# Routing logits by column tiles, one coefficient transpose and an earlier turn of the rows in the second mixture of experts

## The chip, the cores and the metric

The kernel runs on one core of one Trainium2 chip. The metric is device microseconds of one execution. Five engines run their own instruction streams side by side and wait for each other on semaphores: TensorE (PE, with its weight loads shown apart as PEld), VectorE (DVE), ScalarE (ACT), GpSimd (POOL) and SyncE (SP), which issues the transfers.

## The reference

Four layers, each a gated cross-attention and a gated feed-forward block, act on x of 128 sequences of 64 rows of 128 features. The change lies in the feed-forward block of the third layer, a mixture of 8 experts with hidden width 192 of which each row takes two:

```python
xn = _layernorm(x)
logits = xn @ Wr + br
probs = softmax(logits)
topk_probs, topk_idx = top_k(probs, 2)
combine = sum_k topk_probs[:, k] * one_hot(topk_idx[:, k], 8)
for ei in range(8):
    h = gelu(xn @ W1[ei] + b1[ei])
    y = h @ W2[ei] + b2[ei]
    out = out + combine[:, ei:ei + 1] * y
x = x + tanh(g_ffn[2]) * out
```

All 8 experts are computed for every row, and the coefficients (zero but for two) weigh them.

## The kernel before, in words

The 8192 rows lie in SBUF as 64 tiles of 128 rows. Eight stages follow each other, and the stage here, `experts2`, takes the rows in 16 groups of four tiles (512 rows). It is software-pipelined by hand: `steps` runs a body for steps -3 to 15, in which `at(0)` is the group whose outputs are made (g), `at(1)` the one whose hidden units are made (nxt), `at(2)` the one that is routed (far), and `at(3)` the one that is normalised (new). Each engine has such a body, and the order of its instructions is the order in the text.

For one group TensorE does this:

- It turns the four normalised tiles into PSUM (`t_front`, L737). ACT copies the 512 columns into `xTg` (`a_front`, L742).
- Logits (L1667): the turned rows are the weights, the 8 columns of the router's matrix move, once for each tile.
- Hidden units (`hidden`, L1645): 12 chunks of 128 units for 512 rows, three in each quarter of the body. ACT applies gelu (L1808).
- Coefficients: DVE makes scores, softmax, the two best and the coefficients (`scores` and `routing`, L1699 to L1724). PE turns them to 8 rows of 512 in four transposes (L1684), ACT copies them (L1827), SP stores them to DRAM (L1621) and loads them spread over all 128 partitions (L1625, `wide_coef`).
- Weighing: DVE multiplies the hidden units by the spread coefficients (`weigh`, L1736).
- Biases: four matmuls of the 8 turned coefficients by the second biases (L1689), which DVE adds to the rows (`biased`, L1750).
- Outputs (`outputs`, L1655): 12 matmuls for each tile, one tile in each quarter. DVE adds them to the rows (L1782).

On TensorE the quarters of a body are hidden, outputs, hidden, outputs and so on; the logits of far stand ahead of the first quarter, the transposes of its coefficients behind the second outputs, its bias matmuls behind the third, and `t_front` of new behind the fourth. In float32 each matmul shows as two records in the profile, and a transpose as one.

On DVE the body is: scores of far, the outputs of the last group added to x, statistics of new, the first three chunks weighed, new normalised (L205), routing of far, and the other chunks weighed with the bias addition among them. In one step, for far = group 8, `weights3` runs on DVE at the end as well: it unpacks weights of the last stage (L372 to L385).

At the start of a stage each engine waits until the stage before it has updated all its rows. The first steps (`opening` on DVE) have an order of their own.

Stages elsewhere in the kernel that the prediction reads rows from: L485 multiplies 64x64 pieces of weights in `attention0`, with four pieces at different rows and columns of the array; `experts0` (L947, L856) weighs the first mixture with a spread that lies by tiles.

Of the kernel before, what the change touches and what calls it, by code (L numbers as in the profile page):

```python
# [12 lines left out]
ALU = mybir.AluOpType  # L13
ACT = mybir.ActivationFunctionType
AX = mybir.AxisListType
F32 = mybir.dt.float32
# [4 lines left out]
P = 128  # L21
# [60 lines left out]
class Transfers:  # L82
# [6 lines left out]
    def at(self, t):  # L89
        return self.sems[t.par]  # L90
# [1499 lines left out]
def experts2(k, no):  # L1590
# [2 lines left out]
    k.stage_memory()  # L1593
    xTg = [k.take(GCOLS) for _ in range(2)]
    hT = [v.rearrange("p (c n) -> p c n", c=CHUNKS2) for v in (k.take(CHUNKS2 * GCOLS) for _ in range(2))]
    wide_coef = [v.rearrange("p (e n) -> p e n", e=EXPERTS) for v in (k.take(EXPERTS * GCOLS) for _ in range(2))]
    small = lambda: k.take(GROUP * EXPERTS).rearrange("p (j e) -> p j e", j=GROUP)
    score, shifted, expd, hits, coef = small(), small(), small(), small(), small()
    route = Route(k)
    smax, ssum, srec = k.take(GROUP), k.take(GROUP), k.take(GROUP)  # L1600
    coefT = k.take(GCOLS)
    weights3 = Dequantised(k)
    HALF = P // 2
    SCALED = 2 * EXPERTS
    XT, LOGITS, COEFT, HID, NHID, OUT = 0, 1, 2, 3, 3, 6
    s = k.sigs(G, dict(
        l_psum=1, score=1, smax=1, shifted=1, expd=1, ssum=1, srec=1, routing_prob=1, hits=1, coef=1, ct_psum=1,
        ct_sb=1, b2_psum=1, b2_added=1, h_psum=CHUNKS2, h_sb=CHUNKS2, scaled=SCALED, out_psum=1))
    coef_dram = k.nc.dram_tensor("coef_scratch", [G, EXPERTS, GCOLS], F32, kind="Internal").ap()
    coef_stored, coef_spread = k.transfers(G, "coef_stored"), k.transfers(G, "coef_spread")  # L1610
    d_front, p_front, t_front, a_front = group_front(k, f, xTg, XT)
    wide = [P, GROUP, EXPERTS]
# [2 lines left out]
        return k.x[:, bass.ds(g.idx * GROUP, GROUP), :].rearrange("p j n -> p (j n)")  # L1615

    def sync(sp):
        def body(at):
            if g := at(2):
                sp.wait_ge(*s["ct_sb"](g))  # L1620
                sp.dma_start(coef_dram[g.idx], coefT[0:EXPERTS, :]).then_inc(coef_stored.at(g), 16)  # L1621
                sp.wait_ge(*coef_stored(g))
                if g.has(2):
                    sp.wait_ge(*s["scaled"](g.back(2)))
                sp.dma_start(wide_coef[g.par].rearrange("p e n -> p (e n)"),  # L1625
                             coef_dram[g.idx].rearrange("e n -> (e n)").partition_broadcast(P))\
                    .then_inc(coef_spread.at(g), 16)
        steps(sp, G, 2, 0, body)

# [6 lines left out]
    def tensor(pe):  # L1636
        def hidden(g, first):

            for c in range(first, first + 3):
                if c >= NHID:  # L1640
                    pe.wait_ge(*s["h_sb"](g, c - NHID + 1))
                elif g.has(1):
                    pe.wait_ge(*s["h_sb"](g.back(1), CHUNKS2 - NHID + c + 1))
                w = k.w1s[:, c, 0:P] if c < EXPERTS else k.w1tail[:, c - EXPERTS, :]
                pe.matmul(ps[:, HID + c % NHID, :], w, xTg[g.par], start=True, stop=True).then_inc(s["h_psum"].sem, 1)  # L1645

        def outputs(g, j):

            if j == 0 and g.has(2):
                pe.wait_ge(*f["x_updated"](sub(g.back(2), GROUP - 1)))  # L1650
            for c in range(CHUNKS2):
                if j == 0:
                    pe.wait_ge(*s["scaled"](g, c + 1 if c < EXPERTS else EXPERTS + 2 * (c - EXPERTS + 1)))
                w = k.w2a[:, c, :] if c < EXPERTS else k.w2b[:, c - EXPERTS, :]
                mm = pe.matmul(ps[:, OUT + g.par, j * D:(j + 1) * D], hT[g.par][:, c, j * P:(j + 1) * P], w,  # L1655
                               start=c == 0, stop=c == CHUNKS2 - 1)
            if j == GROUP - 1:
                mm.then_inc(s["out_psum"].sem, 1)

        def body(at):  # L1660
            g, nxt, far = at(0), at(1), at(2)
            if far:
                pe.wait_ge(*f["xT_sb"](far))
                if far.has(1):
                    pe.wait_ge(*s["b2_added"](far.back(1)))
                for j in range(GROUP):
                    mm = pe.matmul(ps[:, LOGITS, j * EXPERTS:(j + 1) * EXPERTS], xTg[far.par][:, j * P:(j + 1) * P],  # L1667
                                   k.wr2[:, :], start=True, stop=True)
                mm.then_inc(s["l_psum"].sem, 1)
            if at(3) and not nxt:  # L1670
                t_front(pe, at(3))
            if far and far.idx == 0:
                hidden(far, 0)
            for q in range(GROUP):
                if nxt and (q or nxt.idx):
                    hidden(nxt, 3 * q)
                if g:
                    outputs(g, q)
                if far and q == 1:
                    pe.wait_ge(*s["coef"](far))  # L1680
                    if far.has(1):
                        pe.wait_ge(*s["ct_sb"](far.back(1)))
                    for j in range(GROUP):
                        mm = pe.transpose(ps[0:EXPERTS, COEFT, j * P:(j + 1) * P], coef[:, j], k.ident)  # L1684
                    mm.then_inc(s["ct_psum"].sem, 1)
                if far and q == 2:
                    pe.wait_ge(*s["ct_sb"](far))
                    for j in range(GROUP):
                        mm = pe.matmul(ps[:, LOGITS, j * D:(j + 1) * D], coefT[0:EXPERTS, j * P:(j + 1) * P],  # L1689
                                       k.b2r[:, :], start=True, stop=True)  # L1690
                    mm.then_inc(s["b2_psum"].sem, 1)
            if at(3) and nxt:
                t_front(pe, at(3))
        steps(pe, G, 3, 0, body)

    def vector(dve):
        def scores(g):
            dve.wait_ge(*s["l_psum"](g))
            dve.tensor_tensor(score, ps[:, LOGITS, 0:GROUP * EXPERTS].rearrange("p (j e) -> p j e", j=GROUP),  # L1699
                              k.br2[:, :].unsqueeze(1).broadcast_to(wide), ALU.add).then_inc(s["score"].sem, 1)  # L1700
            dve.wait_ge(*s["score"](g))
            dve.tensor_reduce(smax, score, AX.X, ALU.max).then_inc(s["smax"].sem, 1)
            dve.wait_ge(*s["smax"](g))
            dve.tensor_tensor(shifted, score, smax.unsqueeze(2).broadcast_to(wide), ALU.subtract)\
                .then_inc(s["shifted"].sem, 1)
# [21 lines left out]
        def weigh(g, first):  # L1727

            for c in range(first, first + 3):
                dve.wait_ge(*s["h_sb"](g, c + 1))  # L1730
                if c < EXPERTS:
                    parts = [(slice(0, P), c)]
                else:
                    parts = [(slice(h * HALF, h * HALF + HALF), 2 * (c - EXPERTS) + h) for h in range(2)]
                for rows, e in parts:
                    dve.tensor_tensor(hT[g.par][rows, c, :], hT[g.par][rows, c, :], wide_coef[g.par][rows, e, :],  # L1736
                                      ALU.mult).then_inc(s["scaled"].sem, 1)

        def statistics(g):
            for j in range(GROUP):  # L1740
# [31 lines left out]
        def body(at):  # L1772
            old, nxt, far, new = at(-1), at(1), at(2), at(3)
            if not at(0) and not old:
                opening(at)
                return
            if far:
                scores(far)
            if old:
                dve.wait_ge(*s["out_psum"](old))  # L1780
                dve.wait_ge(*s["b2_added"](old))
                dve.tensor_tensor(rows_of(old), ps[:, OUT + old.par, :], rows_of(old), ALU.add)\  # L1782
                    .then_inc(f["x_updated"].sem, GROUP)
            if new:
                statistics(new)
            if nxt:
                dve.wait_ge(*coef_spread(nxt))
                weigh(nxt, 0)
            if new:
                normalised(new)  # L1790
            if far:
                routing(far)
            if nxt:
                weigh(nxt, 3)
                weigh(nxt, 6)
            if far:
                biased(far)
            if nxt:
                weigh(nxt, 9)
            if far and far.idx == G // 2:  # L1800
                weights3.vector(dve)
        steps(dve, G, 3, 1, body)

    def scalar(act):
# [5 lines left out]

        def body(at):
            nxt, far = at(1), at(2)
            for q in range(GROUP):
                if nxt and (q or nxt.idx):
                    hidden_out(nxt, 3 * q)
# [6 lines left out]
                if far and q == 2:  # L1822
                    act.wait_ge(*s["ct_psum"](far))
                    if far.has(1):
                        act.wait_ge(*coef_stored(far.back(1)))
                        act.wait_ge(*s["b2_psum"](far.back(1)))
                    act.activation(coefT[0:EXPERTS, :], ps[0:EXPERTS, COEFT, :], ACT.Copy).then_inc(s["ct_sb"].sem, 1)  # L1827
            if at(3) and (nxt or not far):
                a_front(act, at(3))
        steps(act, G, 3, 0, body)  # L1830
# [421 lines left out]
```

## Time and profile before

| what | value |
|---|---|
| median of 3 runs | 2160.76 us (2160.32 to 2162.66) |
| the profiled execution's own time | 2156.8 us |
| its span | 2155.0 us |
| TensorE busy | 1918.2 us, 89% |
| VectorE busy | 1670.9 us, 78% |
| ScalarE busy | 1297.6 us, 60% |
| GpSimd busy | 263.6 us, 12% |

The busy share is an average over all eight stages. The stage of the change lies between 1302 and 1717 us of the span, so it is 415 of 2155 us. The median of the runs is 4.0 us above the profiled execution.

### The profile page before, as it was taken

To read this page: it belongs to the slowest core of one execution; us is meant where nothing else is said; L and a number is where in the kernel's file an instruction comes from. 1 tells how busy PE (TensorE), PEld (TensorE's weight loads), DVE (VectorE), ACT (ScalarE), POOL (GpSimd) and SP (SyncE) were. 2 spreads that over 40 slices of the span, in tenths; PEclk is the share of its full clock that TensorE was granted. 3 is DMA by queue.
4 is the path that set the end of the run, shared out by engine and by line. 5 is a ranking of instruction groups with operands and counts; after the bars stand their busy time and mean duration, and the time that the engine had idled before them with its cause. 6 is when DMAs were issued, how large, how long until landed. Compare 5 with 4: busy or idle time off the path is not lost. (4 is left out here: it accounts for less than half of the span.)

```text
span 2155.0 us, 48493 instructions
## 1 busy us (share of the span) xinstructions
PE 1918.2 (89%) x17841; PEld 1473.2 (68%) x17841; DVE 1670.9 (78%) x4752; ACT 1297.6 (60%) x3151; POOL 263.6 (12%) x551
## 2 busy tenths in 40 slices
PE   7999999999969999999999797999999994699608
PEld 6777787787759987777767575777677773344208
DVE  6787787787759979999867797667766488787894
ACT  5777777777742238888866464444455265218744
POOL 1111111111111111111111241000000022100000
PEclk9999999999969999999999898999999997799859
DMA  5222221111125621111100111222222110002452
GB/s 156 52 65 59 53 57 46 44 46 42 42 99 222 237 94 33 33 32 32 24 1 1 30 50 79 80 103 95 79 79 80 50 50 21 0 0 103 179 187 79
DMA packets 115148, 151.60 MB, mean 70 GB/s; under 512 B 45657, under 2 KB 96354, under 8 KB 110818
## 3 DMA queue, kind: packets, MB, share of 16 engines
q1 hardware_dynamic: 111730, 146.91, 21.1%
q8 instruction: 145, 2.38, 0.5%
q10 hardware_dynamic: 3184, 1.58, 0.3%
q14 instruction: 89, 0.73, 0.1%
HBM read 110.18 MB, written 21.50 MB: 61 GB/s over the span
## 5 line engine op out<-in xcount | busy, mean ns | idle before, releaser
L1808 ACT ACTIVATE arena<-banks,b1c 128x512 f32<-128x512 f32 x192 | 131.9, 687 | 166.4 <-PE banks L1645 166.2
L1736 DVE TENSOR_TENSOR arena<-arena 128x512 f32<-128x512 f32 (+1 forms) x256 | 170.5, 686 | 61.5 <-ACT arena L1808 56.4
L624 ACT ACTIVATE arena<-banks,arena 128x128 f32<-128x128 f32 x512 | 180.6, 373 | 1.3 <-DVE arena L570 1.3
L1655 PEld LDWEIGHTS banks<-w2a,arena 128*128 128x128 f32 x1024 | 124.1, 192 | 28.7 <-issue 28.7
L496 PE MATMUL banks<-arena,wk 128*128 128x128 f32 x1024 | 134.0, 285 | 1.2 <-DVE arena L594 1.2
L876 PE MATMUL banks<-we,arena 128*128 128x128 f32 x1024 | 131.5, 285 | 1.5 <-DVE arena L947 0.2
L535 PE MATMUL banks<-wv,arena 128*128 128x512 f32 x256 | 131.9, 597 | 0.0
L496 PEld LDWEIGHTS banks<-arena,wk 128*128 128x128 f32 x1024 | 121.7, 195 | 12.5 <-issue 10.8
L876 PEld LDWEIGHTS banks<-we,arena 128*128 128x128 f32 x1024 | 122.8, 197 | 7.0 <-DVE arena L947 6.2
L1655 PE MATMUL banks<-w2a,arena 128*128 128x128 f32 x1024 | 124.7, 275 | 0.0
L541 PEld LDWEIGHTS banks<-konst,arena 128*128 128x128 f32 x512 | 59.1, 141 | 93.6 <-DVE arena L552 59.0
L1645 PE MATMUL banks<-arena,w1s 128*128 128x512 f32 x256 | 121.8, 609 | 0.0
L624 ACT ACTIVATION_READ_ACCUMULATOR arena<-banks,arena 128x1 f32 x512 | 109.5, 214 | 0.0
L205 DVE TENSOR_SCALAR xhat<-x_tiles,mean_var,rstd 128x128 f32<-128x128 f32 x256 | 79.2, 341 | 34.3 <-POOL rstd L729 27.7
L726 POOL TENSOR_SCALAR var_eps<-mean_var 128x4 f32<-128x4 f32 x96 | 22.1, 231 | 682.3 <-DVE mean_var L706 680.1
L570 DVE TENSOR_REDUCE arena<-banks 128x4 f32<-128x512 f32 x128 | 82.5, 686 | 29.4 <-PE banks L485 29.4
L729 POOL TENSOR_TENSOR rstd<-var_eps,konst 128x4 f32<-128x4 f32 x96 | 100.5, 1047 | 15.2 <-POOL var_eps L726 10.6
L632 ACT ACTIVATE arena<-banks 128x512 f32<-128x512 f32 x64 | 38.2, 597 | 104.0 <-PE banks L496 104.0
L1904 PE MATMUL banks<-konst,local_max 128*1 128x128 f32 (+1 forms) x4 | 1.4, 347 | 111.6 <-DVE local_max L1888 111.6
L552 DVE TENSOR_TENSOR arena<-arena 128x512 f32<-128x512 f32 x128 | 88.6, 692 | 4.4
L541 PE MATMUL banks<-konst,arena 128*128 128x128 f32 x512 | 80.4, 280 | 12.8 <-DVE arena L552 12.7
L1197 ACT ACTIVATE arena<-arena 128x512 f32<-128x512 f32 x128 | 80.7, 630 | 15.9 <-DVE arena L1151 11.4
(246 smaller groups left out, 5023.5 us busy)
## 6 DMA issues: line engine op xcount, KB each, us to landing
arena<-coef_scratch SPq DMA_DIRECT2D x32, 2048.0 KB, 7.2
arena<-arena SPq DMA_DIRECT2D x256, 64.0 KB, 2.0
gated_scratch<-arena SPq DMA_DIRECT2D x16, 768.0 KB, 3.3
arena<-gated_scratch SPq DMA_DIRECT2D x16, 768.0 KB, 4.4
arena<-z1T_scratch SPq DMA_DIRECT2D x128, 64.0 KB, 2.3
arena<-in_ctx_turned SPq DMA_DIRECT2D x32, 256.0 KB, 2.9
arena<-in_ctx SPq DMA_DIRECT2D x64, 64.0 KB, 2.1
z1T_scratch<-arena SPq DMA_DIRECT2D x64, 64.0 KB, 1.6
```

Of the source, the lines that this page charges most:

```text
L496: mm = pe.matmul(ps[:, n, c * P:(c + 1) * P], k.wk0[:, c * P:(c + 1) * P], Z[t.idx % 3][:, :, n], start=True, stop=True)
L535: pe.matmul(ps[:, V0 + b, :], Z[t.idx % 3][:, b].rearrange("p s i -> p (s i)"), k.wv0[:, :], start=True, stop=True).then_inc(s["v_psum"].s ...
L541: mm = pe.transpose(ps[:, b, c * P:(c + 1) * P], prob[:, b, c * P:(c + 1) * P], k.ident)
L552: dve.tensor_tensor(each, each, rec[:, o].unsqueeze(2).broadcast_to([P, HPAIRS, P]), ALU.mult)\
L570: dve.tensor_reduce(low[:, o], ps[:, SCORES + o, :].rearrange("p (c n) -> p c n", c=HPAIRS), AX.X, ALU.max, negate=True).then_inc(s["low"] ...
L624: act.activation(prob[:, o, c * P:(c + 1) * P], ps[:, SCORES + o, c * P:(c + 1) * P], ACT.Exp, bias=low[:, o, c:c + 1], accum_out=total[:, ...
L729: pool.tensor_tensor(k.rstd[:, :, 0], k.ve[:, :, 0], k.konst[:, C_MHALF:C_MHALF + GROUP], ALU.pow).then_inc(f["rstd_ready"].sem, GROUP)
L876: mm = pe.matmul(ps[:, OUT + g.par, j * D:(j + 1) * D], xs[g.par][:, n, j * P:(j + 1) * P], k.we0[:, n, :], start=n == 0, stop=n == EXPERT ...
L1645: pe.matmul(ps[:, HID + c % NHID, :], w, xTg[g.par], start=True, stop=True).then_inc(s["h_psum"].sem, 1)
L1655: mm = pe.matmul(ps[:, OUT + g.par, j * D:(j + 1) * D], hT[g.par][:, c, j * P:(j + 1) * P], w, start=c == 0, stop=c == CHUNKS2 - 1)
L1736: dve.tensor_tensor(hT[g.par][rows, c, :], hT[g.par][rows, c, :], wide_coef[g.par][rows, e, :], ALU.mult).then_inc(s["scaled"].sem, 1)
L1808: act.activation(hT[g.par][:, c, :], ps[:, HID + c % NHID, :], ACT.Gelu, bias=k.b1c[:, c:c + 1])\
```

## The change

Router logits: the router's matrix, widened with zeros to 32 columns (`wr_roomy`), becomes the weights and 128 turned rows move. The four tiles of a group go to four column strips of the array, 32 output partitions each, so that the logits come out turned: expert by row. ACT copies the 128x128 block to SBUF, and a new transpose (`logits_turned`) on PE brings it back to rows by experts. This transpose stands behind the first hidden quarter.

Coefficients: DVE writes them into a 128x128 block (`roomy`) with 32 columns for each tile, whose other columns stay zero. One transpose turns all four tiles.

Biases: `b2_blocks` holds the biases four times on a block diagonal, so that one matmul of 512 columns makes all four tiles. It is filled by four transfers at the stage's start, after DVE has cleared it.

The rows of new are turned ahead of the fourth outputs rather than behind them. On DVE the scores move behind the update of x and the statistics. The store of the coefficients has 128 rows of 512 bytes, and the spread reads four pieces of 4 KB for each partition. The clears and a copy run on DVE at the start of the stage.

```diff
-    wide_coef = [v.rearrange("p (e n) -> p e n", e=EXPERTS) for v in ...]
+    wide_coef = [v.rearrange("p (j e n) -> p e j n", j=GROUP, e=EXPERTS) for v in ...]
+    ROOM = P // GROUP
+    roomy = k.take(P)
+    coef = roomy.rearrange("p (j e) -> p j e", j=GROUP)[:, :, 0:EXPERTS]
+    wr_roomy = k.take(ROOM)
+    b2_blocks = k.take(GCOLS)
+    logitsT = k.take(P)
-    coefT = k.take(GCOLS)
+    coefT = k.take(P)
...
     def sync(sp):
+        sp.wait_ge(cleared, 4)
+        for j in range(GROUP):
+            sp.dma_start(b2_blocks[j * ROOM:j * ROOM + EXPERTS, j * D:(j + 1) * D], k.a["L2_ffn_b2"])\
+                .then_inc(b2_loaded, 16)
...
-                sp.dma_start(coef_dram[g.idx], coefT[0:EXPERTS, :]).then_inc(coef_stored.at(g), 16)
+                sp.dma_start(coef_dram[g.idx], coefT).then_inc(coef_stored.at(g), 16)
...
-                sp.dma_start(wide_coef[g.par].rearrange("p e n -> p (e n)"),
-                             coef_dram[g.idx].rearrange("e n -> (e n)").partition_broadcast(P))\
+                sp.dma_start(wide_coef[g.par].rearrange("p e j n -> p j e n"),
+                             coef_dram[g.idx].rearrange("(j e) n -> j e n", j=GROUP)[:, 0:EXPERTS].partition_broadcast(P))\
...
+        def logits_turned(g):
+            pe.wait_ge(*s["lt_sb"](g))
+            pe.transpose(ps[:, LOGITS, P:2 * P], logitsT, k.ident).then_inc(s["l_psum"].sem, 1)
+
+        pe.wait_ge(cleared, 4)
+        pe.wait_ge(b2_loaded, 16 * GROUP)
...
-                    mm = pe.matmul(ps[:, LOGITS, j * EXPERTS:(j + 1) * EXPERTS], xTg[far.par][:, j * P:(j + 1) * P],
-                                   k.wr2[:, :], start=True, stop=True)
-                mm.then_inc(s["l_psum"].sem, 1)
+                    mm = pe.matmul(ps[j * ROOM:(j + 1) * ROOM, LOGITS, 0:P], wr_roomy, xTg[far.par][:, j * P:(j + 1) * P],
+                                   start=True, stop=True)
+                mm.then_inc(s["lt_psum"].sem, 1)
+                if not nxt:
+                    logits_turned(far)
...
                 if nxt and (q or nxt.idx):
                     hidden(nxt, 3 * q)
+                if far and nxt and q == 0:
+                    logits_turned(far)
+                if nxt and at(3) and q == GROUP - 1:
+                    t_front(pe, at(3))
                 if g:
                     outputs(g, q)
...
-                    for j in range(GROUP):
-                        mm = pe.transpose(ps[0:EXPERTS, COEFT, j * P:(j + 1) * P], coef[:, j], k.ident)
-                    mm.then_inc(s["ct_psum"].sem, 1)
+                    pe.transpose(ps[:, COEFT, 0:P], roomy, k.ident).then_inc(s["ct_psum"].sem, 1)
                 if far and q == 2:
                     pe.wait_ge(*s["ct_sb"](far))
-                    for j in range(GROUP):
-                        mm = pe.matmul(ps[:, LOGITS, j * D:(j + 1) * D], coefT[0:EXPERTS, j * P:(j + 1) * P],
-                                       k.b2r[:, :], start=True, stop=True)
-                    mm.then_inc(s["b2_psum"].sem, 1)
-            if at(3) and nxt:
-                t_front(pe, at(3))
+                    pe.matmul(ps[:, LOGITS, :], coefT, b2_blocks, start=True, stop=True).then_inc(s["b2_psum"].sem, 1)
...
     def vector(dve):
+        dve.memset(roomy, 0.0).then_inc(cleared, 1)
+        dve.memset(b2_blocks, 0.0).then_inc(cleared, 1)
+        dve.memset(wr_roomy, 0.0).then_inc(cleared, 1)
+        dve.wait_ge(cleared, 3)
+        dve.tensor_copy(wr_roomy[:, 0:EXPERTS], k.wr2[:, :]).then_inc(cleared, 1)
+        dve.wait_ge(cleared, 4)
...
-            dve.tensor_tensor(score, ps[:, LOGITS, 0:GROUP * EXPERTS].rearrange("p (j e) -> p j e", j=GROUP),
+            dve.tensor_tensor(score, ps[:, LOGITS, P:2 * P].rearrange("p (j e) -> p j e", j=GROUP)[:, :, 0:EXPERTS],
...
-                    dve.tensor_tensor(hT[g.par][rows, c, :], hT[g.par][rows, c, :], wide_coef[g.par][rows, e, :],
-                                      ALU.mult).then_inc(s["scaled"].sem, 1)
+                    by_tile = hT[g.par][rows, c, :].rearrange("p (j n) -> p j n", j=GROUP)
+                    dve.tensor_tensor(by_tile, by_tile, wide_coef[g.par][rows, e], ALU.mult).then_inc(s["scaled"].sem, 1)
...
-            if far:
-                scores(far)
             if old:
...
             if new:
                 statistics(new)
+            if far:
+                scores(far)
...
             nxt, far = at(1), at(2)
+            if far:
+                act.wait_ge(*s["lt_psum"](far))
+                act.activation(logitsT, ps[:, LOGITS, 0:P], ACT.Copy).then_inc(s["lt_sb"].sem, 1)
...
-                    act.activation(coefT[0:EXPERTS, :], ps[0:EXPERTS, COEFT, :], ACT.Copy).then_inc(s["ct_sb"].sem, 1)
+                    act.activation(coefT, ps[:, COEFT, 0:P], ACT.Copy).then_inc(s["ct_sb"].sem, 1)
```

## Rows read from the trace of the kernel before

**Rows 1.** Windows of the stage: busy time and records by engine, granted clock, DMA:

```profile
1440.00:1465.00 25.00, 24.31 (x145) 18.02 (x144) 16.99 (x53) 12.09 (x18) 1.69 (x2) 1.00 0.21 86
```

**Rows 2.** Timeline of PE over one group: start, busy, line, [idle before]:

```profile
1432.98 1.06 PE L1667 MATMUL banks<-wr,arena 128*128 128x8 f32 x8 [0.69 <-ACT arena L742]
1433.90 2.82 PE L1645 MATMUL banks<-arena,w1s 128*128 128x512 f32 x6
1436.56 1.95 PE L1655 MATMUL banks<-w2a,arena 128*128 128x128 f32 x16
...
1444.49 0.60 PE L1684 MATMUL banks<-konst,arena 128*8 128x128 f32 x4
1444.93 1.88 PE L1645 MATMUL banks<-arena,w1s 128*128 128x512 f32 x4
...
1447.50 1.95 PE L1655 MATMUL banks<-w2a,arena 128*128 128x128 f32 x16
...
1450.27 1.15 PE L1689 MATMUL banks<-b2r,arena 8*128 8x128 f32 x8
1451.36 2.84 PE L1645 MATMUL banks<-arena,w1tail 128*128 128x512 f32 x6
1454.04 1.95 PE L1655 MATMUL banks<-w2a,arena 128*128 128x128 f32 x16
...
1456.71 0.60 PE L737 MATMUL banks<-konst,xhat 128*128 128x128 f32 x4
1458.00 1.06 PE L1667 MATMUL banks<-wr,arena 128*128 128x8 f32 x8 [0.69 <-ACT arena L742]
```

**Rows 3.** Timeline of PE in the first attention, around L485:

```profile
405.09 0.45 PE L485 MATMUL banks<-arena 64*64 64x128 f32 x8
```

**Rows 4.** The same, a longer stretch:

```profile
405.09 1.10 PE L485 MATMUL banks<-arena 64*64 64x128 f32 x32
406.12 2.05 PE L496 MATMUL banks<-arena,wk 128*128 128x128 f32 x16
```

**Rows 5.** Timeline of DVE over the same group as rows 2:

```profile
1434.08 0.19 DVE L1699 TENSOR_TENSOR arena<-banks,br 128x32 f32<-128x32 f32 x1 [1.58 <-PE banks L1667]
...
1434.64 0.69 DVE L1782 TENSOR_TENSOR x_tiles<-banks,x_tiles 128x512 f32<-128x512 f32 x1
...
1436.55 1.86 DVE L1736 TENSOR_TENSOR arena<-arena 128x512 f32<-128x512 f32 x3
1438.79 1.12 DVE L205 TENSOR_SCALAR xhat<-x_tiles,mean_var,rstd 128x128 f32<-128x128 f32 x4 [0.37 <-POOL rstd L729]
...
1442.54 0.25 DVE L1724 SCALAR_TENSOR_TENSOR arena<-arena,gates 128x32 f32<-128x32 f32 x1
```

**Rows 6.** Timeline of ACT, end of the same group:

```profile
1454.24 0.69 ACT L1808 ACTIVATE arena<-banks,b1c 128x512 f32<-128x512 f32 x1 [0.17 <-PE banks L1645]
1457.35 0.60 ACT L742 ACTIVATE arena<-banks 128x512 f32<-128x512 f32 x1 [2.43 <-PE banks L737]
```

**Rows 7.** Groups of instructions by line, costliest first, of DVE, POOL and ACT:

```profile
L1207 ACT ACTIVATE arena<-banks 128x128 f32<-128x128 f32 x64 | 17.8, 277 | 9.8 <-PE banks L1091 9.3
...
L1424 POOL MEMSET arena<- 128x512 f32 x4 | 2.0, 528 | 101.7 <-DVE x_tiles L1782 75.8 <-DVE x_tiles L1327 25.9
```

**Rows 8.** One line's instructions, L947: duration min/median/max in ns:

```profile
L947 DVE TENSOR_TENSOR arena<-arena x128: 680/684/693, 635.4 to 776.5; 128x512 f32<-128x512 f32 x128
```

**Rows 9.** Timeline of SP, the spread of the same group:

```profile
1450.35 0.33 SPq L1625 DMA_DIRECT2D arena<-coef_scratch  x1
```

**Rows 10.** DMA issues: tiles, count, KB each, median us to landing:

```profile
arena<-coef_scratch SPq DMA_DIRECT2D x32, 2048.0 KB, 7.2
...
out_x<-x_tiles SPq DMA_DIRECT2D x4, 1024.0 KB, 5.1
```

**Rows 11.** Timeline of PE after the step with the unpacking of weights:

```profile
1522.11 0.60 PE L1684 MATMUL banks<-konst,arena 128*8 128x128 f32 x4 [2.41 <-DVE arena L1724]
```

**Rows 12.** Timeline of DVE in the opening, the first weighing:

```profile
1324.50 1.89 DVE L1736 TENSOR_TENSOR arena<-arena 128x512 f32<-128x512 f32 x3 [1.45 <-DMA arena<-coef_scratch]
```

More of the change, by code:

```diff
@@ L1595, in experts2 @@
     hT = [v.rearrange("p (c n) -> p c n", c=CHUNKS2) for v in (k.take(CHUNKS2 * GCOLS) for _ in range(2))]
-    wide_coef = [v.rearrange("p (e n) -> p e n", e=EXPERTS) for v in (k.take(EXPERTS * GCOLS) for _ in range(2))]
+    wide_coef = [v.rearrange("p (j e n) -> p e j n", j=GROUP, e=EXPERTS) for v in (k.take(EXPERTS * GCOLS) for _ in range(2))]
     small = lambda: k.take(GROUP * EXPERTS).rearrange("p (j e) -> p j e", j=GROUP)
-    score, shifted, expd, hits, coef = small(), small(), small(), small(), small()
+    score, shifted, expd, hits = small(), small(), small(), small()
+    ROOM = P // GROUP
[4 more added lines that the diff above has]
+    logitsT = k.take(P)
     route = Route(k)
     smax, ssum, srec = k.take(GROUP), k.take(GROUP), k.take(GROUP)
-    coefT = k.take(GCOLS)
+    coefT = k.take(P)
     weights3 = Dequantised(k)
@@ L1606, in experts2 @@
     s = k.sigs(G, dict(
-        l_psum=1, score=1, smax=1, shifted=1, expd=1, ssum=1, srec=1, routing_prob=1, hits=1, coef=1, ct_psum=1,
+        lt_psum=1, lt_sb=1, l_psum=1, score=1, smax=1, shifted=1, expd=1, ssum=1, srec=1, routing_prob=1, hits=1, coef=1, ct_psum=1,
         ct_sb=1, b2_psum=1, b2_added=1, h_psum=CHUNKS2, h_sb=CHUNKS2, scaled=SCALED, out_psum=1))
-    coef_dram = k.nc.dram_tensor("coef_scratch", [G, EXPERTS, GCOLS], F32, kind="Internal").ap()
+    cleared, b2_loaded = k.sem("L2_cleared"), k.sem("L2_biases_loaded")
+    coef_dram = k.nc.dram_tensor("coef_scratch", [G, P, P], F32, kind="Internal").ap()
     coef_stored, coef_spread = k.transfers(G, "coef_stored"), k.transfers(G, "coef_spread")
```

## The prediction

> **What bounds the kernel now.** I read the windows first, to see which engine sets the pace of this stage. In the 25 us from 1440 TensorE is busy for 24.31 us at granted clock 1.00 (2.4 GHz), VectorE for 17.0 and ScalarE for 12.1 [rows 1]. The other windows between 1340 and 1640 us look the same but for one, so PE sets the pace and a microsecond off PE's stream is one off the group. Next comes PE's timeline over one group, from logits to logits: 1432.98 to 1458.00, or 25.02 us [rows 2]. I take it apart by the starts of its blocks. Three hidden chunks with nothing odd beside them take 2.57 us (1444.93 to 1447.50), and outputs of one tile 2.67 (1454.04 to 1456.71). Four of each make 21.0 us, which the change leaves alone. The other 4.0 us are what it works on:
>
> - logits: 0.92 us, and the hidden quarter behind them takes 2.66 rather than 2.57; together 1.00;
> - the four transposes of coefficients: 0.44;
> - the bias matmuls: 1.09, with 0.10 more in the outputs ahead (1447.50 to 1450.27) and 0.11 in the hidden quarter behind (1451.36 to 1454.04); together 1.30;
> - the turned rows: 1.29 from the transposes at 1456.71 to the logits at 1458.00, of which 0.69 is the wait for ACT's copy, named in the last row of the group.
>
> Last come DVE's and ACT's timelines, for what else could be late: DVE waits 1.58 us for the logits [rows 5], and ACT's copy has an idle ahead of it, waiting for PE [rows 6].
>
> **The change part by part.**
>
> The turned rows. The four transposes stay; four in a row cost 0.44 (the coefficients' four in [rows 2]). Moved ahead of the fourth outputs, they leave 2.67 us of outputs to hide the copy. ACT is then in the last gelus: the last starts 0.20 us and ends 0.89 us after the hidden quarter (1454.24 plus 0.69, against 1454.04), and the copy takes 0.60 [rows 6]; it ends some 1.6 us after the hidden quarter, while PE arrives at the logits after 0.44 + 2.67 = 3.1 us. So 1.29 becomes 0.44: 0.85 saved. If only the named wait went, it would be 0.69. New's normalised rows are ready at 1439.9 (1438.79 plus 1.12, [rows 5]), long before. Behind the moved transposes stand only the outputs, whose operands are ready. 13 steps (0 to 12) have this slot.
>
> The coefficients. One transpose instead of four: 0.11 for 0.44, 0.33 saved in 14 steps (0 to 13). The three that go have no other effect, and the weight is 128 columns wide as in the turned rows, which cost 0.11 as well.
>
> The biases. One matmul of 512 columns is two records; six take 2.57, so two 0.86. The slot was 1.30, so 0.44 saved in 14 steps. The bounds: 0.2 if the small extras on either side stay, 0.44 if they go. I take the upper end, since such an extra shows beside every block with a narrow tile in this group and beside no full one.
>
> The logits. Eight records again, of 128 columns instead of 8. One after another at 0.11 they would take 0.88. The nearest row to four strips of the array at once is L485: eight records of 128 columns each, on four pieces of the array, span 0.45 us from the first start to the last end [rows 3], where eight starts 0.11 apart would span more than 0.88. 32 of them take 1.03 us to the next block's start [rows 4], 0.032 each; in batches of four that start 0.107 apart, eight batches are 0.86, and 0.17 is left as the price of going in and out. Eight records in strips are then two batches, 0.21, with 0.17 and about 0.1 in the quarter beside them: 0.5. To this comes one transpose, 0.11. So 1.00 becomes 0.61: 0.39 saved in 14 steps. The bounds are 0.36 (saves 0.64) and, if the strips run one after another, 0.88 + 0.28 + 0.11 = 1.27 (loses 0.27). I stay near L485, since a strip differs from its pieces only in depth.
>
> A rule of the Trainium skill speaks against this part: by TensorEngine Tiling (Array Packing), section Instruction Overhead, a matmul costs about 60 cycles however few columns move. The old eight records of 8 columns would be 0.2 us by it (an estimate: 8 times 60 cycles at 2.4 GHz), less than the new ones, and the logits would lose 0.33 a group instead of saving 0.39, a sum of 15.2 instead of 25.3. The trace has 0.92 for them [rows 2], so the rule's price isn't theirs here; their 128-column weights have to be loaded.
>
> The copy of the turned logits on ACT is new: 0.28 by a copy of that size [rows 7]. ACT has 12.9 us of idle in 25 [rows 1], and does it while PE is in the first hidden chunk, 0.86 us long. The new transpose waits for it only behind three chunks.
>
> The scores come later. They start 2.48 us before the second block, the outputs at 1436.56 [rows 2, 5]; the transpose now ends at that block, so they start about 0.2 after it begins, 2.7 later. In exchange the update of x and the statistics (1434.64 to 1436.55, 1.91 us) run ahead of them, in the idle of 1.58 and beyond, and the 0.37 for GpSimd's rstd goes [rows 5]. The coefficients are thus 0.4 later against PE. They were ready at 1442.79, 1.70 before their transpose at 1444.49; 1.3 us of slack stay. Costed at nothing; without the cover every microsecond costs one.
>
> Weighing. Its third operand is now read in four pieces. The first mixture does just this in 684 ns [rows 8]; here three took 1.86 [rows 5]. Nothing.
>
> The spread. Four pieces of 4 KB a partition instead of one of 16. It was issued at 1450.35 and lands 7.2 later, at 1457.6 [rows 9, 10]; DVE first reads it a group on, at 1461.6. By the new order DVE reads it 15.9 after the coefficients' transpose rather than 17.1, so 2.8 us of slack stay. The longest that the pieces make it: out_x moves 1024 KB in 512-byte pieces in 5.1 us [rows 10], so 2048 KB in 10.2. That would eat it and 0.2 of the slack above. Nothing, in steady state.
>
> The opening. Three clears and a copy on DVE come before the first statistics. A clear of 512 columns took 0.53 on GpSimd [rows 7]; I take 1.1 for the four with their waits, 0.5 to 1.5 as bounds. SP issues four loads of biases behind them, and PE waits for these before its first transposes, which wait for about 4 us of normalising anyway. The opening ends with the first spread, for which DVE waits [rows 12]; it comes 1.1 later, PE's shorter blocks give a little back. 1.0 lost, and 3 more if the spread in pieces takes as long as out_x makes possible.
>
> The step after the unpacking. There PE waits 2.41 us for coefficients [rows 11]. DVE sets that step's end, so what PE saves on the way (0.85 and 0.39) is not gained, but for the 0.37 of rstd: about 1.0 lost.
>
> The sum: 13 x 0.85 = 11.1; 14 x (0.33 + 0.44 + 0.39) = 16.2; less 1.0 and 1.0: 25.3 us. The profiled execution took 2156.8 us, so 2131.5 for one like it; the median of the runs lies 4.0 above it, which gives 2135.5.
>
> **The rivals.**
>
> *The strips run one after another.* For: nothing here shows weights 128 rows deep and 32 columns wide in strips. Against: [rows 3], with eight records in 0.45. The logits lose 0.27 instead of saving 0.39, 14 x 0.66 = 9.2: 2144.7.
>
> *The copy still comes late.* If ACT reaches it only after the fourth outputs, the 0.85 stays: 2135.5 + 11.1 = 2146.6. Against: the 1.5 us between the copy's end and PE's arrival. This would be the change not doing what it says.
>
> *DVE takes over.* If scores to coefficients take 2 us longer than I make it, 0.7 a group goes past the slack, 9 us over 13 groups: 2144.6. For: 1.3 us is the tightest slack here. Against: every piece of the chain has its row.
>
> *The spread late, the one that ends slower.* The slacks of the spread and the coefficients add up to 4.1 us, so landing above 11.3 us costs a microsecond a group; from 13.3 (25.3 over 13 is 1.95) the kernel is slower than before. At 14 it is 2.7 x 13 = 35 lost: 2170.6. For: four times the pieces. Against: out_x's 10.2.
>
> **How the numbers follow.** Measurement tells a difference of about 0.2% (4.3 us) from none. I give my forecast 0.71, its own range 2130 to 2143; the strips 0.11, the late copy 0.04, DVE 0.07, the late spread 0.04, and 0.03 that several shortfalls meet within 0.2%. Faster 0.93, same 0.03, slower 0.04. The range: at the low end the logits at 0.36 (3.5 more) and an opening at nothing (1.0 more), 2131, with 2 us for the median's scatter, 2129; at the high end the strips and the late copy, 2147.
>
> **What would show it.** The turned rows' block ahead of the fourth outputs with no wait at the logits; a group of 23.0 us; the logits' block at about 0.5; two bias records in 0.86; PE with no wait for L1724's coefficients but in the step after the unpacking, there about 3.3 us. The prediction is wrong if a wait for coefficients or for the spread shows in every group, or if the logits' eight records start 0.11 apart.

## The result and the profile after

The changed kernel takes 2142.5 us (median of 4 runs, 2140.7 to 2144.1) against 2161.7 for the kernel before beside it: a ratio of 0.990, 95% interval 0.9884 to 0.9915, so 18 to 25 us less. Forecast were 25.3 us less and 2135.5; the range was 2129 to 2147.

The stage itself can be read more closely than the whole. From the last update of x by the stage ahead to its own last update, one profiled execution gives 415.4 us before (1301.65 to 1717.1) and 393.9 after (1302.85 to 1696.8): 21.5 less. PE's timeline over one group after (line numbers are the new ones; L1686 is the logits in strips, L1674 their transpose, L1708 the one transpose of coefficients, L1711 the biases):

```profile
1429.30 0.43 PE L1686 MATMUL banks<-arena 128*32 128x128 f32 x8
1429.66 2.84 PE L1657 MATMUL banks<-arena,w1s 128*128 128x512 f32 x6
1432.34 0.27 PE L1674 MATMUL banks<-konst,arena 128*128 128x128 f32 x1
1432.45 1.95 PE L1667 MATMUL banks<-w2a,arena 128*128 128x128 f32 x16
...
1440.38 0.27 PE L1708 MATMUL banks<-konst,arena 128*128 128x128 f32 x1
1440.49 1.88 PE L1657 MATMUL banks<-arena,w1s 128*128 128x512 f32 x4
...
1443.07 1.95 PE L1667 MATMUL banks<-w2a,arena 128*128 128x128 f32 x16
...
1445.75 1.02 PE L1711 MATMUL banks<-arena 128*128 128x512 f32 x2
1446.61 2.74 PE L1657 MATMUL banks<-arena,w1tail 128*128 128x512 f32 x6
1449.18 0.60 PE L737 MATMUL banks<-konst,xhat 128*128 128x128 f32 x4
1449.62 1.95 PE L1667 MATMUL banks<-w2a,arena 128*128 128x128 f32 x16
...
1452.39 0.43 PE L1686 MATMUL banks<-arena 128*32 128x128 f32 x8
```

From logits to logits it is 23.09 us now, 25.02 in [rows 2]. The wait ahead of the logits is gone, and every extra can be read off: strips 0.36 (1429.30 to 1429.66), with 0.10 in the hidden quarter behind them and 0.10 in the outputs ahead (2.77 from 1449.62); a transpose 0.11; one more for the coefficients 0.11; biases 0.86, with nothing beside them; the turned rows 0.44. The window over the group shows PE busy for all of it, at granted clock 1.00 (columns as in [rows 1]):

```profile
1429.30:1452.39 23.09, 23.09 (x137) 16.46 (x136) 17.02 (x54) 11.98 (x18) 1.21 (x2) 1.00 0.29 94
```

DVE's timeline of that group: it waits 1.05 us for the turned logits and has the coefficients at 1439.0 (1438.76 plus 0.25), 1.4 us ahead of their transpose; before it was 1.7 [rows 2, 5].

```profile
1432.65 0.19 DVE L1724 TENSOR_TENSOR arena<-banks,br 128x32 f32<-128x32 f32 x1 [1.05 <-PE banks L1674]
...
1438.76 0.25 DVE L1749 SCALAR_TENSOR_TENSOR arena<-arena,gates 128x32 f32<-128x32 f32 x1
```

So the groups do what was forecast, within 0.1 us each. What is short of 25.3 in the stage lies at two other places. One is the step after the unpacking of weights, against [rows 11]. PE's timeline there, and windows around it:

```profile
1512.62 0.47 PE L1708 MATMUL banks<-konst,arena 128*128 128x128 f32 x1 [2.81 <-DVE arena L1749]
1512.89 3.19 PE L1657 MATMUL banks<-arena,w1s 128*128 128x512 f32 x4
...
1516.78 1.95 PE L1667 MATMUL banks<-w2a,arena 128*128 128x128 f32 x16
```

```profile
1508.00:1512.00 4.00, 1.81 (x17) 1.62 (x15) 3.57 (x24) 2.25 (x4) 0.31 (x1) 1.00 0.02 6
1512.00:1516.00 4.00, 3.38 (x6) 1.59 (x7) 2.73 (x7) 0.69 (x1) 0.00 (x0) 0.57 0.00 0
1516.00:1520.00 4.00, 4.00 (x29) 3.28 (x28) 2.32 (x4) 1.54 (x3) 0.00 (x0) 1.00 0.05 16
```

PE waits 2.81 us, and the hidden quarter behind the wait takes 3.89 (1512.89 to 1516.78) where all others take 2.58: the granted clock is 0.57 in those 4 us, most of them at the lower level, 1.2 GHz. Before, behind 2.41 us of wait [rows 11], it had stayed at 1.00, and the quarter took 2.57. The kernel before:

```profile
1522.00:1526.00 4.00, 3.89 (x18) 2.39 (x19) 3.25 (x6) 2.05 (x4) 0.00 (x0) 1.00 0.00 0
```

The other is the opening. DVE's timeline there shows the four new instructions, 0.99 us from the first start to the statistics (1303.91); SP's and DVE's show the first spread, issued at 1320.54 and used at 1329.12:

```profile
1302.92 0.17 DVE L1715 MEMSET arena<- 128x128 f32 x1
1303.14 0.48 DVE L1716 MEMSET arena<- 128x512 f32 x1
1303.59 0.09 DVE L1717 MEMSET arena<- 128x32 f32 x1
1303.70 0.17 DVE L1719 COPY arena<-wr 128x8 f32<-128x8 f32 x1
...
1329.12 6.22 DVE L1762 TENSOR_TENSOR arena<-arena 128x512 f32<-128x512 f32 x10 [2.82 <-ACT arena L1833]
```

```profile
1320.54 0.39 SPq L1637 DMA_DIRECT2D arena<-coef_scratch  x1
```

The bracket names ACT, but what DVE needs of ACT for its first chunks was done by 1318.8; the spread is what came at 1329.1, 8.6 us after its issue. Over the stage, one line's transfers:

```profile
DMA to landing us min/median/max: 8.3/8.8/9.4
```

With the spread in one piece it was 7.2 over both mixtures [rows 10], and 6.7 for the first one of this stage.

The opening differs in its clock as well. The first hidden quarter, from its start to the first transpose of coefficients, took 3.79 us before at a granted clock of 0.68, and 4.80 after at 0.53:

```profile
1310.84:1314.63 3.79, 3.79 (x8) 1.48 (x8) 3.15 (x25) 3.23 (x4) 0.00 (x0) 0.68 0.01 2
```

```profile
1313.07:1317.87 4.80, 4.80 (x7) 1.92 (x7) 3.53 (x28) 3.25 (x4) 0.20 (x1) 0.53 0.01 2
```

### The profile page after: what moved, and what is told of

It reads as the page before. It is cut to its first block and busy times, and to the rows that moved or that the text cites. A ratio compares the mean times of both kernels' runs of the same rounds, so it can differ in the third digit from the quotient of the medians.

```text
span 2138.9 us, 48262 instructions
## 1 busy us (share of the span) xinstructions
PE 1902.3 (89%) x17713; PEld 1448.2 (68%) x17713; DVE 1670.6 (78%) x4756; ACT 1295.8 (61%) x3167; POOL 257.8 (12%) x551
## 5 line engine op out<-in xcount | busy, mean ns | idle before, releaser
L1975 PE MATMUL banks<-arena,wup 128*128 128x512 f32 x192 | 92.2, 618 | 0.8 <-ACT arena L2133 0.8
```

The costliest lines, as they stand in the source:

```text
L1975: pe.matmul(ps[:, 1 + CHUNKS3 * n + c, :], w[:, c, :], xdT[:, g.idx, :], start=True, stop=True)\
```

## The experiments

All kernels below compute the whole reference. Total times of one kernel scatter by 3 to 12 us, so each is also taken apart by PE's timeline: the stage, the time from its start to the logits of step 0, step 0, the steps 1 to 6 and 8 to 12 (all alike to 0.01), step 7 behind the unpacking, and the rest from the logits of step 13. The times are us, each from one profiled execution but the first column.

| kernel | median of runs | stage | to step 0 | step 0 | a step | step 7 | rest |
|---|---|---|---|---|---|---|---|
| before | 2161.7 | 415.4 | 31.27 | 25.01 | 25.02 | 27.59 | 56.40 |
| changed | 2142.5 | 393.9 | 33.36 | 23.83 | 23.09 | 27.53 | 55.25 |
| changed, again | 2140.1 | 394.0 | 33.54 | 23.83 | 23.09 | 27.48 | 55.21 |
| only the rows turned ahead | 2148.8 | 406.9 | 32.55 | 24.17 | 24.07 | 29.18 | 56.32 |
| all but the rows turned ahead | 2148.9 | 401.9 | 33.67 | 24.59 | 23.84 | 26.11 | 55.30 |
| logits as before | 2139.6 | 398.7 | 33.99 | 25.09 | 23.32 | 27.56 | 55.59 |
| unpacking in thirds | 2134.7 | 390.8 | 33.74 | 24.78 | 23.09 | 23.09 | 55.26 |
| part of it a step earlier | 2133.6 | 391.9 | 33.82 | 24.78 | 23.09 | 24.09 | 55.28 |
| clears on GpSimd | 2138.5 | 395.7 | 33.21 | 23.82 | 23.09 | 29.44 | 55.30 |
| coefficients side by side | 2131.4 | 391.7 | 31.27 | 23.78 | 23.09 | 27.47 | 55.25 |
| that, and thirds | 2131.5 | 387.9 | 32.54 | 23.09 | 23.09 | 23.09 | 55.25 |
| that, thirds, clears on GpSimd | 2130.3 | 386.5 | 30.97 | 23.23 | 23.09 | 23.09 | 55.28 |

The medians of the kernel before, run beside the others, were 2160.5 to 2161.5.

**The changed kernel again.**

> The changed kernel once more. In its first profile the stage takes 394.0 us (before: 415.5) and all other stages together 1744.9 (before: 1739.5). Theory: the others are unchanged and the 5.4 us are scatter between executions; then the others lie at 1738 to 1743 here and the run near 2141. Rival: the change slows the stages behind it; then the others lie at 1744 to 1746 again.

The other stages took 1744.7 us again, as the rival has it. But over all twelve profiles they take from 1736.5 to 1745.0, and the part ahead of this stage, whose text no edit touches, ends anywhere from 1297.4 to 1305.5. The kernel with clears on GpSimd has 1743.5, the one with the coefficients side by side 1736.5, with the same text behind the stage. So a difference of 5 us outside is within what unrelated edits bring; the rival is not shown, and why two profiles of one kernel agree so well is open.

**One part alone, and all but that part.** In the kernel before:

```diff
                 if nxt and (q or nxt.idx):
                     hidden(nxt, 3 * q)
+                if nxt and at(3) and q == GROUP - 1:
+                    t_front(pe, at(3))
                 if g:
                     outputs(g, q)
...
-            if at(3) and nxt:
-                t_front(pe, at(3))
```

> The kernel before with one part of the change alone, the rows of new turned ahead of the fourth outputs. Theory: 0.85 us a group over 13 groups, less what the step after the unpacking takes back (0.85): 10.2 us less than before, about 2151, and a group of 24.17 us. Rival, that ACT's copy is late anyway: about 2161.

And the reverse in the changed kernel:

> The changed kernel with the rows of new turned behind the fourth outputs again. Theory, the parts are independent: 0.85 x 13 less 0.85 in the step after the unpacking, so 10 us more than the changed kernel, about 2152.5, and a group of 23.95 us. Rival, the parts overlap (DVE sets the pace once PE is shorter, so that the turn ahead gives less): under 6 us more.

Alone the turn ahead saves 0.95 a step, more than the 0.85 forecast; on top of the other parts 0.75. The other parts give 1.18 without it (25.02 to 23.84), for a forecast 1.16. So the parts add up to within 0.2 and DVE doesn't take over: the rival of overlap falls. PE's timeline of the turn ahead alone shows where the difference comes from:

```profile
1429.67 0.96 PE L1667 MATMUL banks<-wr,arena 128*128 128x8 f32 x8
1430.48 2.82 PE L1645 MATMUL banks<-arena,w1s 128*128 128x512 f32 x6
```

With no wait ahead of them the old logits take 0.81 to the next block (0.92 behind a wait in [rows 2]), so 0.11 went with the wait. The strips have 0.10 in the outputs ahead of them, and those stand there only when the rows are turned earlier.

The turn ahead shortens the whole stage by 8.5 alone and by 7.9 on top, rather than 10. Alone, its time to step 0 is 1.3 longer, with neither clears nor pieces: a hidden quarter there took 4.08 us for 2.68, at a granted clock of 0.65. And step 7 goes the other way: 29.18 with the turn ahead alone, where PE waits 3.36 us for coefficients and the clock falls, and 26.11 in the kernel with all but it, where PE waits 2.05 and the clock stays.

**The logits as before, in the changed kernel.**

```diff
-                    mm = pe.matmul(ps[j * ROOM:(j + 1) * ROOM, LOGITS, 0:P], wr_roomy, xTg[far.par][:, j * P:(j + 1) * P],
-                                   start=True, stop=True)
-                mm.then_inc(s["lt_psum"].sem, 1)
+                    mm = pe.matmul(ps[:, LOGITS, P + j * ROOM:P + j * ROOM + EXPERTS], xTg[far.par][:, j * P:(j + 1) * P],
+                                   k.wr2[:, :], start=True, stop=True)
+                mm.then_inc(s["l_psum"].sem, 1)
...
```

> The changed kernel with the logits as before (8 columns move, no strips, no copy on ACT, no second transpose), the scores still behind the statistics on DVE. Theory: the slot was 1.00 and is now 0.67 (0.36, 0.20 in the blocks beside it and 0.11), so 0.33 more in each of 12 steps, about 4 us more than the changed kernel, 2146.5; the coefficients come 2.7 us earlier, so the step after the unpacking is not shorter, since DVE sets it. Rival, that the strips cost PE more than they save elsewhere: no more than the changed kernel.

A step takes 23.32, 0.23 more than in strips, and the stage 4.7 more, of which 1.9 lie in the opening and step 0. The runs show nothing of it (2139.6), as the other stages took 8 us less in its profile: at this size only the stage tells. The strips pay, but by 0.23 a step and not by 0.39: the old logits without a wait ahead cost 0.90 (0.81 and 0.09 in the quarter behind), not 1.00, and the strips 0.67. Step 7 is no shorter, as expected; PE waits 2.57 us there, and the clock falls behind it as in the changed kernel.

**The unpacking in thirds, and part of it a step earlier.**

```diff
-            if far and far.idx == G // 2:
-                weights3.vector(dve)
+            if far and far.idx == G // 2 - 1:
+                weights3.scales(dve)
+            if far and far.idx == G // 2:
+                weights3.rounded(dve)
+            if far and far.idx == G // 2 + 1:
+                weights3.rescaled(dve)
...
```

The three methods hold the instructions of the old one in their order.

> The changed kernel with the unpacking of the last stage's weights on DVE cut in three parts of 1.5 to 2.0 us, one in each of three steps. DVE has 1.05 us of idle ahead of the scores and 1.4 of slack at the coefficients, 2.4 together. Theory: no part makes PE wait, so the wait of 2.81 us goes, and with it the 1.27 by which the hidden quarter behind it ran long at a granted clock that had fallen (3.85 for 2.58): 4.1 us less than the changed kernel, about 2138.4. Rival, that the slow quarter has another cause than the wait: 2.8 less, and a quarter of 3.85 stays somewhere.

The second has `rescaled` in the same step as `rounded`.

> The changed kernel with the first part of the unpacking (1.9 us: the maxima, their scaling, the reciprocals) one step earlier, the rest where it was. Theory: the wait for coefficients shrinks from 2.81 to 0.9 us, and the clock does not fall behind it, so 1.9 + 1.27 = 3.2 us less than the changed kernel. Rival, the clock falls whatever the wait's length: 1.9 less and a hidden quarter of 3.85 behind it.

In thirds step 7 is a step like the others, 23.09: 4.4 less. With only the scales earlier it is 24.09, 3.4 less, of which the wait gives 2.0. PE's timeline there:

```profile
1511.61 0.33 PE L1715 MATMUL banks<-konst,arena 128*128 128x128 f32 x1 [0.78 <-DVE arena L1756]
1511.78 1.88 PE L1664 MATMUL banks<-arena,w1s 128*128 128x512 f32 x4
...
1514.35 1.95 PE L1674 MATMUL banks<-w2a,arena 128*128 128x128 f32 x16
```

Behind 0.78 us of wait the hidden quarter takes 2.57 again, so the theory that the long wait cost 1.3 us more than itself holds, and the rival falls. Yet both stages gained less, 3.1 and 2.0, since their step 0 and what is ahead of it took 1.3 more. In thirds, PE's timeline there is this:

```profile
1333.89 0.42 PE L1693 MATMUL banks<-arena 128*32 128x128 f32 x8 [2.28 <-DVE x_tiles L1782]
1334.24 4.52 PE L1664 MATMUL banks<-arena,w1s 128*128 128x512 f32 x6
```

The logits of step 0 wait for the bias addition, which stands on DVE behind the chunks that wait for the first spread. In the changed kernel that wait was 1.87 and the quarter behind it 2.68; here it was 2.28 and 4.31. With only the scales earlier the wait was 2.04 and the quarter 4.19. No edit touches the text of the opening in these two.

**The clears on GpSimd.** The four instructions go from the start of `vector` to the start of `gpsimd`, and DVE waits for them ahead of its first coefficients.

> The changed kernel with the three clears and the copy at the stage's start on GpSimd instead of DVE. Theory: the statistics start 1.04 us earlier and the whole opening with them: 1.0 less than the changed kernel, the stage 393.0. Rival, that the loads of biases (behind the clears) or GpSimd's own rstd behind them hold the opening up: no less.

The statistics do start at once, and PE's first transposes come 4.32 us into the stage instead of 5.31. But the second group's transposes are only 0.7 earlier, the coefficients' transpose 0.4 (the hidden quarter ahead of it took 5.12 us for 4.81, both at a lowered clock), the first weighing 0.15, and the logits of step 0 0.15 to 0.33. The expectation of 1.0 was wrong; the stage is 1.8 longer, not 1.0 shorter. Step 7, where PE waits 3.14 us, takes 1.9 more than in the changed kernel, which makes up that difference.

**The coefficients side by side.**

```diff
-    roomy = k.take(P)
-    coef = roomy.rearrange("p (j e) -> p j e", j=GROUP)[:, :, 0:EXPERTS]
+    close = k.take(COLS)
+    coef = close.rearrange("p (j e) -> p j e", j=GROUP)
...
-                             coef_dram[g.idx].rearrange("(j e) n -> j e n", j=GROUP)[:, 0:EXPERTS].partition_broadcast(P))\
+                             coef_dram[g.idx].rearrange("(j e) n -> j e n", j=GROUP).partition_broadcast(P))\
...
-                    pe.transpose(ps[:, COEFT, 0:P], roomy, k.ident).then_inc(s["ct_psum"].sem, 1)
+                    pe.transpose(ps[0:COLS, COEFT, 0:P], close, k.ident).then_inc(s["ct_psum"].sem, 1)
...
```

> The changed kernel with the coefficients side by side (32 columns), turned to 32 rows, stored as 32 rows and spread in one piece of 16 KB a partition, as before; the bias block has its rows to match and zeros behind them, so that its matmul stays as it is. Theory: the spread lands in 7.0 to 7.2 us instead of 8.3 to 8.8, which only the opening feels: 1.6 less than the changed kernel, and the group stays at 23.09. Rival, that the opening is held up by something else (the gelus, the clock): no less although the spread lands sooner.

The spreads of this stage land in a median of 7.1 us (8.8 in the changed kernel). SP's and DVE's timelines of the opening:

```profile
1314.89 0.36 SPq L1638 DMA_DIRECT2D arena<-coef_scratch  x1
```

```profile
1322.03 6.22 DVE L1763 TENSOR_TENSOR arena<-arena 128x512 f32<-128x512 f32 x10 [1.84 <-DMA arena<-coef_scratch]
```

The first weighing starts 24.2 us into the stage instead of 26.3; 1.5 of the 2.1 is the landing (7.1 for 8.6), the rest an earlier issue. The logits of step 0 are back at 31.27, as before the change, although the clears are still there. A step stays at 23.09, so the pieces cost nothing in steady state.

The edit isn't shown to give all of that back. The first hidden quarter took 3.75 us here, at a granted clock of 0.69, where the changed kernel took 4.80 at 0.53, and that is what made the issue earlier. In the kernel that has the unpacking in thirds as well, the next one below, the same opening has that quarter in 4.98 at 0.51. The two windows:

```profile
1308.04:1311.79 3.75, 3.75 (x7) 1.49 (x7) 3.14 (x24) 3.22 (x4) 0.00 (x0) 0.69 0.01 2
```

```profile
1309.19:1314.17 4.98, 4.98 (x7) 1.84 (x7) 3.52 (x28) 3.26 (x4) 0.20 (x1) 0.51 0.01 2
```

So the fairer pair is the two kernels with thirds, with pieces and without: the quarter takes 4.78 and 4.98, and both issue the first spread 17.7 us into the stage. In one piece it lands in 7.0 for 9.0, the first weighing starts 1.9 earlier, and the logits of step 0 come 1.2 earlier (32.54 for 33.74), where they then wait for ACT's copy and no longer for DVE.

The runs are 9 to 11 us under the changed kernel, of which the stage explains 2.2. The other stages took 8 less in the profile, and why is open.

**Put together.**

> The changed kernel with both: coefficients side by side and spread in one piece of 16 KB, and the unpacking in three parts. Theory, the two are independent: logits of step 0 at 31.3 us into the stage, 23.8 for that step, twelve groups of 23.09 with no wait among them, a tail of 55.25: a stage of 387.4, against 394.0 as changed, and 2140.1 less 6.6, about 2134. Rival, that the spread in pieces and the unpacking cost the same microseconds (the granted clock in the opening decides): a stage over 390.

387.9 for 387.4, with no wait for coefficients in step 7: the two are independent. The opening splits otherwise (32.54 and 23.09 for 31.3 and 23.8), with the same sum to 0.5.

> The same with the clears on GpSimd as well. With the clears alone on GpSimd the statistics began 1.0 us earlier in the stage, but its logits of step 0 only 0.15 to 0.33. Theory, that the hidden quarters of the opening, which ran longer there at a lower granted clock (5.3 and 4.1 for 5.0 and 2.7), took the rest: here 386.4 to 387.2, no more than 1 us under the one without it. Rival, the whole microsecond shows: 386.4.

The stage takes 386.5, 1.4 under the one without it, more than the theory allowed and what the rival had named. But the first hidden quarter took 4.23 here for 4.98, so whether the clears or the clock gave it isn't settled. The runs show 2130.3 us: 0.985 of the kernel before (95% 0.9828 to 0.9877), some 10 us under the changed kernel's 2140 to 2143. The runs can't tell it from the one without the third edit.

## Why the prediction was right, and where it was off

- *The turned rows:* right. 0.44 with no wait; 0.95 alone, 0.75 beside the strips, for 0.85. The prediction gave the 0.11 that the old logits lose with the wait to the logits. That the copy comes late, a rival, is refuted by the missing wait.
- *Coefficients:* right, 0.11 for 0.44.
- *Biases:* right at the upper end, 0.86 with nothing beside it. The small extras did belong to the narrow tiles.
- *Logits:* over-sized. The slot is 0.67 for a forecast 0.61, since strips cost 0.10 on either side, and what it replaces is 0.90 once the wait is gone, not 1.00: 0.23 a step by the experiment, for 0.39. The rival of strips one after another is refuted, as their eight records leave PE after 0.36.
- *Scores later:* right, 1.4 us of slack for a forecast 1.3. DVE did not take over.
- *The spread:* it landed in 8.8 (median), not 7.2, within the bound of 10.2 from out_x, and was hidden in steady state. The late spread, the rival that ends slower, did not come.
- *The opening:* mis-sized. 1.0 was forecast; it lost 2.1 by the logits of step 0, and step 0 itself saved 1.2 instead of 2.0, as PE waits 0.52 us in it for coefficients. The clears delay the first transposes by the 1.0 that they were given. Left at nothing in the sum were the landing in pieces, 1.9 longer for the first spread, of which 1.2 reaches the logits of step 0 in the pair with thirds, and the granted clock: the first hidden quarter took 1.0 more. How the 2.1 divides among the three isn't settled, since the clock of the opening differs from kernel to kernel.
- *The step after the unpacking:* mis-sized. PE's wait grew by 0.4, to 2.81 and not to the forecast 3.3, yet the step gained 0.06 instead of 1.0: the granted clock fell behind the wait and the next quarter took 1.3 more. The prediction had priced the wait alone, and too high; the clock, which outweighed that, it had left out.

In sums: eleven steps at 1.93 are 21.2, step 0 1.2, step 7 0.1, the rest 1.15, the opening -2.1: 21.5 of the forecast 25.3 in the stage. The runs show 19.2, with an interval that holds 21.5; the difference is no larger than what the other stages scatter by.

## What to carry to other kernels

Price the opening and the odd step of a pipelined stage by themselves: here the steady steps gave what their rows promised, and nearly all of the shortfall came from places that run once. A transfer whose longer landing is hidden in the steady steps can be on the path of the first. Where an edit shortens the engine that sets the pace, a stall that another engine ends grows (by all of the 0.95 with the turn ahead alone, by 0.4 in the whole change), and can cost more than its length. And before a difference in an opening is put down to an edit, the granted clock of the two openings has to be compared.

## What the runs showed of the hardware

Weights of 128 rows and 32 columns in four column strips of the array do run at once in float32: eight records of 128 columns start and make room for the next block in 0.36 us, where eight at the 0.11 of a transpose here would need 0.88.

The granted clock in this dense stage was 1.00 behind waits of 0.78, 2.05 and 2.41 us in step 7. Behind 2.57, 2.79 to 2.81, 3.14 and 3.36 it fell, to means of 0.50 to 0.66 between the transpose and the next outputs, a stretch that took 1.4 to 2.7 us more. At the logits of step 0 it stayed at 1.00 behind waits of up to 1.87 and one of 2.08, and fell behind 2.04, 2.28 and 2.82, where the next quarter took 4.2 to 4.4 us for 2.68. So the length of the wait alone doesn't decide. The Trainium skill, TensorE: Matmul & The Clock Gate, section Part 1: The HAM clock gate, says that the clock has two levels and falls to 1.2 GHz when PE has been idle; these rows agree, as each of these falls stands behind idle time. What else decides isn't settled by them.
